# A conv block and a windowed graph block in fp32: third gathers moved, small products packed on TensorE

## The reference, cut to what matters

```
# block 1
h = depthwise_conv7x7(x) + conv_b                   # per channel
h = (h - mean_c(h)) * rsqrt(var_c(h) + eps) * ln_g + ln_b
h = gelu(h @ w1 + b1) @ w2 + b2                     # 24 -> 96 -> 24 channels
x1 = h * layer_scale + x

# block 2
y = (x1 * fc1 + fc1_b) * fc1_s + fc1_t              # 24 -> 24, 1x1
nodes = y cut into windows of 8 x 8 pixels: 64 nodes of 24 values each
xn = nodes / |nodes|
idx = the 9 nearest nodes of each node by |xn_i - xn_j|^2   (the node itself is one)
feat = [node_i, node_j - node_i]                    # 48 values for each neighbour j
h = gelu((feat @ ew + eb) * es + et)                # 48 -> 48
h = max over the 9 neighbours
out = ((h @ fc2 + fc2_b) * fc2_s + fc2_t) + x1      # 48 -> 24, 1x1
```

## Time and profile before

| | before |
|---|---|
| runs without a profile | 2035.86, 2036.62, 2038.4 us |
| the profiled execution, its own time | 2036.98 us |
| its span, first to last instruction | 2035.2 us |
| TensorE (matmul rows) | 1882.2 us, 92% |
| VectorE | 1504.8 us, 74% |
| ScalarE | 1057.6 us, 52% |
| GpSimd | 782.7 us, 38% |
| mean granted TensorE clock, share of 2.4 GHz | 0.954 |

### The profile page before, as it was taken

The page is one execution under the profiler, slowest core; times in us unless marked ns, Lnnn a source line. Parts: engine busy times, 40 slices in busy tenths (PEclk is TensorE's granted clock), DMA queues, the critical chain, the costliest instruction groups (busy, mean ns, idle before and its releaser), DMA issues.

```text
span 2035.2 us, 47073 instructions
## 1 busy us (share of the span) xinstructions
PE 1882.2 (92%) x16042; PEld 872.5 (43%) x16042; DVE 1504.8 (74%) x5840; ACT 1057.6 (52%) x2574; POOL 782.7 (38%) x463
## 2 busy tenths in 40 slices
PE   5997999999888999999999999999999999999996
PEld 2443555555433444444444444444444444444432
DVE  4222223222249999999998999999999999999997
ACT  0001444444445666666665666666666666656663
POOL 3001444444413343444443444444444444434432
PEclk9998999999969999999998999999999999999998
DMA  7884233333310111111111111111111111111100
GB/s 143 149 146 97 75 90 93 100 93 94 98 32 24 38 38 38 38 38 38 38 38 38 38 38 38 38 38 38 38 38 38 38 35 40 38 38 26 26 21 15
DMA packets 154565, 111.62 MB, mean 55 GB/s; under 512 B 117504, under 2 KB 144384, under 8 KB 154240
## 3 DMA queue, kind: packets, MB, share of 16 engines
q1 hardware_dynamic: 154368, 109.04, 21.9%
HBM read 57.61 MB, written 32.11 MB: 44 GB/s over the span
## 4 chain that ended last, share of the span: by engine, by line
PE 68%; DVE 17%; ACT 10%; issue 3%; SPq 1%; DMA 1%; POOL 0%; POOLq 0%; ACTq 0%
PE bank L1088 14%; DVE red L806 8%; PE bank L890 8%; PE bank L941 6%; PE bank L1018 5%; PE bank L1043 5%; PE bank L949 5%; DVE onehot L793 4%; PE bank L915 3%; PE bank L1059 3%; PE bank L1028 3%; PE bank L1052 2%; PE bank L988 2%; PE bank L981 2%; PE bank L924 2%
## 5 line engine op out<-in xcount | busy, mean ns | idle before, releaser
L806 DVE TENSOR_REDUCE red<-bank 128x64 f32<-128x512 f32 x1176 | 757.2, 689 | 100.7 <-PE bank L1088 91.0
L535 ACT CAST pb<-bank 64x192 bf16<-64x192 f32 x1176 | 367.5, 313 | 416.8 <-PE bank L1059 391.6
L1088 PE MATMUL bank<-onehot,pb 128*32 128x512 bf16 x7056 | 511.6, 397 | 7.6 <-DVE red L806 7.5
L378 POOL TENSOR_TENSOR hq<-red,arena 128x384 f32<-128x384 f32 x196 | 220.0, 1123 | 379.0 <-DVE red L806 377.5
L359 POOL TENSOR_TENSOR rs<-ve,mhalf 112x16 f32<-112x16 f32 x56 | 162.4, 2899 | 350.7 <-DVE ve L712 350.7
L793 DVE TENSOR_SCALAR onehot<-slot 128x256 bf16<-128x256 bf16 x1568 | 251.0, 240 | 0.0
L1088 PEld LDWEIGHTS bank<-onehot,pb 128*32 128x32 bf16 x7056 | 136.9, 97 | 182.9 <-issue 96.2
L890 PE MATMUL bank<-arena,toep 120*120 120x448 f32 x384 | 161.1, 581 | 21.4 <-DVE arena L644 21.4
L1028 PE MATMUL bank<-arena,wqs 128*128 128x448 f32 x336 | 170.9, 593 | 9.6 <-DMA arena<-yb 6.0
L370 POOL TENSOR_TENSOR rn<-nv,mhalf 128x28 f32<-128x28 f32 x28 | 134.6, 4805 | 114.4 <-DVE nv L765 79.6
L785 DVE MATCH_REPLACE8 marked<-t,bank 128x64 bf16<-128x64 f32 x784 | 160.5, 223 | 0.0
(11 more groups left out here) (93 smaller groups left out, 2511.2 us busy)
## 6 DMA issues: line engine op xcount, KB each, us to landing
x_d<-x1o SPq DMA_DIRECT2D x28, 448.0 KB, 2.8
ht<-x_d SPq DMA_DIRECT2D x28, 448.0 KB, 3.7
arena<-in_x SPq DMA_DIRECT2D x24, 392.0 KB
ht<-conv_d SPq DMA_DIRECT2D x112, 84.0 KB
xt<-in_x SPq DMA_DIRECT2D x112, 84.0 KB
xt<-x_d SPq DMA_DIRECT2D x112, 84.0 KB
arena<-yb SPq DMA_DIRECT2D x168, 56.0 KB, 2.0
arena<-yb SPq DMA_DIRECT2D x56, 168.0 KB, 2.7
```

The lines of the kernel that those rows point to most:

```text
L378: nc.gpsimd.tensor_tensor(hq[:, :, :, :], red[:, k, :, :, :], qs[:, b, :, wx, :].unsqueeze(1).broadcast_to([128, 2, T, NN]), ALU.add).then ...
L535: last = nc.scalar.copy(pb[64 * u:64 * u + 64, k, part, :, :, u, :], src[64 * u:64 * u + 64, :, :, :])
L806: nc.vector.tensor_reduce(red[:, k, h, t, :], src, axis=mybir.AxisListType.X, op=op).then_inc(s["red_done"], 1)
L1088: last = mm(bank[32 * q:32 * q + 32, (k + t) % 2, :], pb[:, k, part, g, c, :, :].rearrange("p u o -> p (u o)"), onehot[:, k, g, :, :].rear ...
```

## The change

The changed kernel does these things.

1. *Gather tiles.* A gather now makes one of the three chunks of 16 output channels for all four groups; before, the first three tiles were three chunks of one group and the fourth part collected one chunk of the last group. The count of products stays 12. The layouts of the node terms and of the weights of `fc2` follow from it.
2. *Node terms.* Three calls an iteration instead of six; each is 8 products of a 64 x 32 tile, four groups of output partitions times two halves of the contraction rows. The lower half makes the `qs` term in bank 5, the upper the `gs` term in bank 7. ScalarE takes both after each call. `y2` is loaded by 16 transfers.
3. *fc2.* Three times four products of 64 x 64, all in column 4, into banks 6 and 7.
4. *expand* in the block stage: the middle tile as two products of 128 rows and 64 output columns, the other two as four of 64 x 64. `variance` uses blocks of 128 pixels, two products of 64 weight columns each. `contract` takes the tiles in the order 1, 0 and 1, 2.
5. *Order.* In a step of the block stage `turn_std`, `centre` (now four ahead) and `variance` come before `contract` and `expand`. In a column of the graph stage the third gather comes after `ranks` and after the side work that stood behind it. `fc1` is made wholly in column 5; y is squared in the middle of ScalarE's column 6.

TensorE in two steps of the block stage, before. L915 is `centre`, L941 `expand`, L932 `turn_std`, L924 `variance`, L949 `contract`; a row of ISA or REGISTER_ALU is a wait or a count.

The core of the diff:

```diff
-LB = L // NBLK
+LB = 128
...
-        QS_AT = (((), (0,)), ((1,), (2,)), ((3,), (4,)), ((), ()), ((), ()), ((), ()), ((), (5,)))
+        FC1_BANKS = (6, 7)
+        QS_AT = (((), ()), ((0,), ()), ((), (1,)), ((), ()), ((), ()), ((), ()), ((), (2,)))
...
+                    sp.wait_ge(s["y_done"], 2 * i + (u + 1))
+                    for g in range(G):
+                        for h in range(2):
+                            sp.dma_start(y2[64 * h + 32 * u:64 * h + 32 * u + 32, b, g, :],
+                                         yb[32 * g:32 * g + 32, b, u, :, :].rearrange("c w i -> c (w i)")
+                                         ).then_inc(y2_in[b], 16)
...
+                for t in (1, 0, 2):
+                    act.wait_ge(mm1_d, 3 * m + (1 if t == 1 else 3))
...
+            def take_qs(i, b, t):
+
+                act.wait_ge(s["qs_mm"], T * i + (t + 1))
+                at_least(act, s["addq_done"], WX * (i - 1))
+                nc.scalar.activation(qs[:, b, t, :, :].rearrange("p w i -> p (w i)"), bank[:, 5, 0:L], ACT.Identity,
+                                     bias=gb[:, t:t + 1], scale=1.0).then_inc(s["qs_done"], 1)
+                at_least(act, s["og_done"], WX * (i - 1))
+                nc.scalar.activation(gs[:, b, t, :, :].rearrange("p w i -> p (w i)"), bank[:, 7, 0:L], ACT.Gelu,
+                                     bias=gb[:, t:t + 1], scale=1.0).then_inc(s["qs_done"], 1)

             def act_slot(n, i, j, r, gather=True, add=True, ahead1=True, ahead2=True, pre=True, post=True, early=True):
                 wx, b = r % WX, r // WX
                 if ahead1:
                     split(n + 1, (r + 1) % 2, 0, s["p_mm"], s["hi_done"])
                 if early and wx == 6:
-                    make_y(i + 2, b, us=(0,))
+                    make_y(i + 2, b, us=(1,), banks=FC1_BANKS)
+                if pre and wx == 3:
+                    spread_xa(i + 1, (b + 1) % 2, 1)
                 if ahead1:
                     split(n + 1, (r + 1) % 2, 1, s["res1_mm"], s["mid_done"])
+                if early and wx == 6:
+                    square_y(i + 2, b)
                 if pre:
                     for e in QS_AT[wx][0]:
                         take_qs(i + 1, (b + 1) % 2, e)
...
                     nc.scalar.copy(mts[:, :], bank[:, 4, 0:G * NN]).then_inc(s["mts_done"], 1)
                 if ahead1:
                     split(n + 1, (r + 1) % 2, 2, s["res2_mm"], s["lo_done"])
-                if early and wx == 6:
-                    make_y(i + 2, b, us=(1,))
                 if pre and wx == 3:
                     take_xb(i + 1, (b + 1) % 2, 0)
                 if add:
                     act.wait_ge(s["addq_done"], n)
                     at_least(act, s["mx_done"], n - 1)
                     nc.scalar.activation(gg[:, :, :, :], hq[:, :, :, :], ACT.Gelu).then_inc(s["geg_done"], 1)
+                if pre and wx == 3:
+                    take_xb(i + 1, (b + 1) % 2, 1)
                 if pre:
                     for e in QS_AT[wx][1]:
                         take_qs(i + 1, (b + 1) % 2, e)
...
                                    ).then_inc(s["slot_done"], 1)
                 if pre and wx == 2:
                     square_xa(i + 1, (b + 1) % 2)
-                if pre and wx in (2, 3):
-                    spread_xa(i + 1, (b + 1) % 2, wx - 2)
+                if pre and wx == 2:
+                    spread_xa(i + 1, (b + 1) % 2, 0)
                 if pre and wx == 1:
                     for h in range(2):
                         take_norm(i + 1, h)
-                if pre and wx == 3:
-                    take_xb(i + 1, (b + 1) % 2, 1)
                 if post and wx in (4, 5):
                     fc2_leave(i - 1, (b + 1) % 2, j, wx - 4)
-                if early and wx == 6:
-                    square_y(i + 2, b)
+                if early and wx == 5:
+                    make_y(i + 2, b, us=(0,), banks=FC1_BANKS)
...
+                    for half in range(2):
+                        a = min(LB * k + 64 * half, L - 64)
+                        last = mm(bank[64 * half:64 * half + 64, 2, G * k:G * k + G], sq[:, a:a + 64], P("mean4"),
+                                  start=True, stop=True)
...
             def expand(m, r):
                 pe.wait_ge(hn_d, m + 1)
-                for t in range(3):
-                    at_least(pe, gelu_d, 3 * (m - 1) + (t + 1))
-                    mm(bank[:, 3 + t, 0:L], w1g[:, t, :], hn[:, r % 2, :], start=True, stop=True).then_inc(mm1_d, 1)
+                for c in range(2):
+                    last = mm(bank[64 * c:64 * c + 64, 4, 0:L], w1g[:, 1, 64 * c:64 * c + 64], hn[:, r % 2, :],
+                              start=True, stop=True)
+                last.then_inc(mm1_d, 1)
+                for k, t in ((0, 0), (64, 2)):
+                    for c in range(2):
+                        last = mm(bank[64 * c:64 * c + 64, 3 + t, 0:L], w1g[k:k + 64, t, 64 * c:64 * c + 64],
+                                  hn[k:k + 64, r % 2, :], start=True, stop=True)
+                last.then_inc(mm1_d, 2)

             def contract(m, r):
                 at_least(pe, x1_dn, m - 1)
-                pe.wait_ge(gelu_d, 3 * m + 2)
-                for half, t in ((0, 0), (1, 1), (0, 1), (1, 2)):
-                    if t == 2:
-                        pe.wait_ge(gelu_d, 3 * m + 3)
+                for half, t in ((0, 1), (1, 1), (0, 0), (1, 2)):
+                    pe.wait_ge(gelu_d, 3 * m + (1 if t == 1 else 3))
                     last = mm(bank[64 * half:64 * half + 64, 6 + r % 2, 0:L], w2s[:, t, 64 * half:64 * half + 64],
-                              gl[:, t, :], start=t == half, stop=t == half + 1)
+                              gl[:, t, :], start=t == 1, stop=t != 1)
                 last.then_inc(mm2_d, 1)

             def mlp_slot(m, r, j, first=False):

                 end = NSTEP if isinstance(m, int) else 1 << 30
                 now = m if isinstance(m, int) else 0
+                if now + 1 < end:
+                    turn_std(m + 1, r + 1)
+                if now + 4 < end:
+                    centre(m + 4, r + 4, j + (r + 4) // NBUF)
+                if now + 3 < end:
+                    variance(m + 3)
                 if not first:
                     contract(m - 1, r - 1)
-                if now + 3 < end:
-                    centre(m + 3, r + 3, j + (r + 3) // NBUF)
                 expand(m, r)
...
+            def fc2(i, b):
+                pe.wait_ge(s["og_done"], WX * (i + 1))
+                at_least(pe, s["xb_done"], 2 * min(i + 3, NI))
+                for t in range(T):
+                    for h in range(2):
+                        for gp in range(2):
+                            last = mm(bank[64 * h:64 * h + 64, 6 + gp, 0:L],
+                                      f2[64 * gp:64 * gp + 64, t, 64 * h:64 * h + 64],
+                                      og[64 * gp:64 * gp + 64, b, t, :, :, :].rearrange("p r w c -> p (r w c)"),
+                                      start=t == 0, stop=t == T - 1)
+                last.then_inc(s["fc2_mm"], 2)
+
+            def node_terms(i, b, old, t):
+
+                if t == 0:
+                    pe.wait_ge(y2_in[b], 16 * 4 * G * (old + 1))
+                at_least(pe, s["qs_done"], 2 * T * i + 2 * t)
+                if i == 0:
+                    pe.wait_ge(s["xb_done"], 2)
+                elif t == 1:
+                    pe.wait_ge(s["rnt_done"], 2 * (i + 1))
+                elif t == 2:
+                    pe.wait_ge(s["y_done"], 2 * min(i + 2, NI))
+                for g in range(G):
+                    for h, bk in ((0, 5), (1, 7)):
+                        last = mm(bank[32 * g:32 * g + 32, bk, 0:L], wqs[64 * h:64 * h + 64, t, :],
+                                  y2[64 * h:64 * h + 64, b, g, :], start=True, stop=True)
+                last.then_inc(s["qs_mm"], 1)
...
-                        g, c = (t, q) if q < NCH else (T, t)
                         last = mm(bank[32 * q:32 * q + 32, (k + t) % 2, :],
-                                  pb[:, k, part, g, c, :, :].rearrange("p u o -> p (u o)"),
-                                  onehot[:, k, g, :, :].rearrange("p k i -> p (k i)"), start=part == 0, stop=part == 2)
+                                  pb[:, k, part, q, t, :, :].rearrange("p u o -> p (u o)"),
+                                  onehot[:, k, q, :, :].rearrange("p k i -> p (k i)"), start=part == 0, stop=part == 2)
                 last.then_inc(s["gat_mm"], 1)
...
                 if post and wx == 4:
-                    fc2(i - 1, bn, 0)
-                if post and wx == 5:
-                    fc2(i - 1, bn, 1, (1,))
-                if early and wx == 6:
-                    fc1(i + 2, b, j + 1, 1)
+                    fc2(i - 1, bn)
                 for e in qa:
                     node_terms(i + 1, bn, j + b, e)
                 if ahead2:
                     transpose(n + 2, k)
                 if ahead1:
```

(11 more changed lines are left out.)

144 lines of the change are left out of this document (45 added, 99 removed).

## The result

| | before | after |
|---|---|---|
| median without a profile | 2036.24 us (2034.37 to 2038.4) | 2172.23 us (2170.96 to 2176.17) |
| span of the profiled execution | 2035.2 us | 2170.3 us |
| first reduction of the graph stage at | 588.0 us | 555.0 us |
| from there to the end | 1447.2 us | 1615.3 us |
| one iteration | 51.45 us | 58.03 us |

The ratio of after to before is 1.0675, with a 95% interval of 1.0652 to 1.0698: 6.7% slower. TensorE does 96 us less, and the kernel takes 135 longer. In an iteration of the changed kernel in which the clock doesn't fall, column 5 is 9.25.

What follows compares the result with a forecast made beforehand. It took TensorE to bound the block stage, and TensorE and VectorE, nearly full and coupled by waits, the graph stage: 2036.98 - 48 (block stage) + 136 (graph stage) = 2125 us, own range 2100 to 2155, 8 in 10 2088 to 2190.

Steps and rivals of the forecast that it cites:

- the block stage gains less: Rival, block stage: a new wait (gelu before contraction, or dear variance) adds 20 to 40 us, 2150 to 2165; 5%.
- the clock (2180, 11%): Rival, graph stage: idle places in columns 5, 6 and 0 make the clock fall about once more an iteration; 2180, 11%.
- Block stage, 48 saved: Block stage: a step falls from 6.13 to 5.26 us through expand and variance, 56 times, 48 us saved.
- the row tiles overlap: Block stage, expand: products on different rows of the array run side by side, 1.50 us for 2.25.
- The column rule, third gather's start + 3.12: Graph stage: with a late third gather, a column lasts its start, counted from the distances, + 3.12 us; otherwise 6.53.
- Columns 6 and 0: Graph stage: column 6 takes 8.06 us, its ranks behind the square of y; column 0, gather not late, 6.6.
- The clock, 0.2 us an iteration: Graph stage: clock seldom falls at the norms, but TensorE idles in two places of most columns; + 0.2 us an iteration.
- the wait of 0.65 at column 0: Graph stage, before the norms: TensorE's 0.65 us wait for ScalarE's square goes, the square being ready half a column earlier.
- The onehot row, 0.5 us: Graph stage, column 2: one-hot row of 2.71 us instead of 1.17 in about half the iterations; + 0.5 us.
- Packs: Graph stage side work: a pack of node terms takes 0.83 us, the fc2 pack of column 4 takes 2.41.
- packs a third dearer: Graph stage: estimate from the skill's page on row tiles, some 60 us more in all, 2185.
- VectorE stays the bound: Rival, graph stage: the late third gather is hidden, columns fall to 6.53 to 6.9 us; about 1895 to 1960, 8%.

Runs made afterwards that it cites:

- e5: Changed kernel with the fourth product of turn_std over all 128 rows instead of 64, as an ordinary product instead of a transpose: 2163.4 us, ratio 1.0613.
- e6: Changed kernel with expand again as three products of 128 x 128 weights, in the order 1, 0, 2: 2203.71 us, ratio 1.0821.
- e1: Changed kernel with the third gather back directly behind the second subtraction, ahead of ranks and side work: 1980.66 us, ratio 0.9729.
- e2: Changed kernel with the third gather behind the ranks but ahead of the side work: 2085.16 us, ratio 1.0237.
- e10: Changed kernel with two useless 448-column products an iteration filling TensorE's idle time, in columns 5 and 6: 2135.64 us, ratio 1.0497.
- best2: Changed kernel, third gather early, fc2 split, second fc1 product in column 6, halfsq's third product behind ranks, 128-row turn_std, GpSimd's second scaling behind the one-hot matrix: 1943.47 us.
- best3: The kernel of best2 with halfsq's third product ahead of the marks of column 3 again: 1931.37 us, ratio 0.9481.

## Why the prediction was right, and where its sizes were off

The forecast was 2125, the measured median 2172: the sign and the mechanism held, two sizes did not. The median lies outside the forecast's own range, 2100 to 2155, to which 66% was given, and inside the wide one, 2088 to 2190. The excess of 47 us is 15 ahead of the graph stage and 32 in it: two rivals in part, that the block stage gains less (2150 to 2165, 5%) and the clock (2180, 11%).

- *Block stage, 48 saved.* 33 were, 29 of them in the 56 steps (5.61 us for a forecast of 5.26). Expand 1.66 for a forecast of 1.50, variance 0.56 for 0.50, contract 1.56 for 1.65: small. The term that was mis-sized is `turn_std`: the prediction kept its 0.39, and the row shows 0.68. It counted one change of tiling in the step, 0.08, and did not look at the fourth transpose, which has 64 rows between products of 128; e5 and e6 show 0.17 that goes with it and 0.15 for coming behind the 64 x 64 tiles. That the row tiles overlap was right.
- *The column rule, third gather's start + 3.12.* Right. In column 5 the start is 6.14 and the column 9.25; in columns 1 to 5 the forecasts 8.49, 7.17, 8.13, 8.20 and 9.29 met 8.51, 7.28, 8.11, 8.34 and 9.25, where the clock doesn't fall. e1 shows that the gather's place is the cause, e2 how it divides.
- *Columns 6 and 0.* Forecast 8.06 and 6.6; measured 9.09 and 7.35. With the clock kept up (e10) they are 8.26 and 6.84, near the forecast. So the longest of VectorE's waits for the third gather is in column 6 (2.82), not in column 5 as expected (2.63).
- *The clock, 0.2 us an iteration.* This is the other mis-sized term: 1.42 (58.03 less the 56.61 of e10, which has no fall). The forecast was 56.6. The prediction named this as a rival and was led away from it by the norms: the wait of 0.65 at column 0 did go and no fall begins there any more, but the fall moved to columns 5 and 6, behind waits that the prediction had on its list of idle places and priced at 0.2.
- *The onehot row, 0.5 us.* Not seen after the change: column 2 is 7.28 in all iterations. The sum of the columns without a fall came out 0.67 above the forecast 55.94 (0.1 to 0.2 each in columns 0, 2, 4 and 6). That these two errors nearly cancel is luck.
- *Packs.* Forecast 0.83 and 2.41; measured 0.92 (1084.31 to 1085.23) and 2.41 (1108.21 to 1110.62), changes of tiling included. The prediction's estimate from the Trainium skill, TensorE: Matmul & The Clock Gate (Part 3), where row tiles gain less than their number, was packs a third dearer; the rows show at most 0.1 us over the forecast, and the measurement decides.
- *The rivals.* "VectorE stays the bound" (1895 to 1960) is where best2 and best3 arrive (1943, 1931): it needed the gather in its old place, and e1 with that alone stops at 1981.

Left open: why columns 1, 3 and 5 of e1 still stand above VectorE's 6.53 was not taken apart, the wait for bank 7 in column 6 of best2 and best3 was not removed, and no run has the packed products of the graph stage without the changes of order, so that their own worth is not known.

## What to carry to other kernels

Where two engines hand work back and forth, the place of the product that the other engine waits for last can be worth more than the savings beside it: here 96 us less work on TensorE, and 192 us lost by one product's place, 38 of them through the clock. Put side work behind what the other engine waits for, and before moving an instruction past a bank's reader look up who writes that bank next. When a wait of TensorE goes away, look at whether the fall of its clock goes too, or only moves to the next place where it idles.

## What the runs showed of the hardware

- A useless product can shorten a kernel: two fillers of 0.8 us an iteration saved 1.42, because the clock stayed at 2.4 GHz in all of iterations 3 to 25 (mean granted clock of the execution 0.982 in e10, 0.964 after). One filler alone moved the fall in half of the iterations: the product behind the wait of 1.06 took 1.86 instead of 1.02.
- With a transpose of 64 rows between products of 128 rows a step was 0.17 us longer than with a product of 128 rows in its place (e5). Transposes of 128 rows behind tiles of 64 x 64 took 0.15 longer than behind full-width products (e6).
- A one-hot group on VectorE (bf16, eight instructions, 1.16) took 1.96 while a GpSimd instruction with two fp32 inputs ran. The one-hot rows of 2.71 us in the earlier trace rows are the same: at 1067.64 two such instructions of GpSimd ran one after the other beside it. The Trainium skill, GPSIMD Engine Reference (Specifications), says that the two engines share their interfaces to SBUF and disturb each other for some forms of VectorE's instructions; the trace agrees, and the price, 0.80 us for one overlap, is the rows'; GpSimd's own instruction hardly differs (1.11 beside the one-hot group, 1.05 behind it).
